# Recommendation head on one core: the last batch tile begins nine units later, label rows and two kinds of loads move

## What is computed

```python
h = concat([q1, q2]) @ w5 + b5
f6 = h @ w6 + b6
g = (v @ v.T)[iu, ju]
f7 = (h[:, iu] * h[:, ju] * g) @ w7 + b7
out8 = concat([f6, f7]) @ w8 + b8
return einsum('bu,bku->bk', out8, label_embedding)
```

## Time and profile before

| | us |
|---|---|
| median of 3 runs | 1762.22 (1760.65 to 1764.42) |
| the profiled execution | 1760.75 |
| its span | 1758.9 |
| TensorE busy | 1583.0 (90% of the span) |
| VectorE busy | 1421.1 (81%) |
| ScalarE busy | 996.4 (57%) |
| GpSimd busy | 137.9 (8%) |
| moved by DMA | 615.20 MB, 350 GB/s over the span |

### The profile page before, as it was taken

The page is one execution under the profiler, slowest core; times in us unless marked ns, Lnnn a source line. Parts: engine busy times, 40 slices in busy tenths (PEclk is TensorE's granted clock), DMA queues, the critical chain, the costliest instruction groups (busy, mean ns, idle before and its releaser), DMA issues.

```text
span 1758.9 us, 25341 instructions
## 1 busy us (share of the span) xinstructions
PE 1583.0 (90%) x7086; PEld 1159.8 (66%) x7086; DVE 1421.1 (81%) x5487; ACT 996.4 (57%) x2931; POOL 137.9 (8%) x96
## 2 busy tenths in 40 slices
PE   2889999999999999999999999899999999998700
PEld 1467677677777777777777777577777777765400
DVE  8897888873898999799998986567777668678956
ACT  7665777764565646464655644344444444433497
POOL 5000000000000000000000000000000000003366
PEclk9999999999999999999999999899999999999955
DMA  7799877977899999999999899999999989999898
GB/s 295 268 390 369 288 273 242 330 279 258 299 332 388 364 409 354 413 357 370 392 359 395 324 393 383 413 358 328 359 381 374 334 314 406 350 357 406 329 397 361
DMA packets 170385, 615.20 MB, mean 350 GB/s; under 512 B 20784, under 2 KB 49421, under 8 KB 162053
## 3 DMA queue, kind: packets, MB, share of 16 engines
q1 hardware_dynamic: 106469, 368.44, 55.0%
q10 hardware_dynamic: 61696, 242.33, 37.0%
q0 software_dynamic: 2080, 2.81, 0.5%
HBM read 609.70 MB, written 3.79 MB: 349 GB/s over the span
## 4 chain that ended last, share of the span: by engine, by line
PE 66%; DMA 15%; DVE 11%; ACT 4%; issue 2%; POOL 1%; SPq 1%; ACTq 0%; DVEq 0%; POOLq 0%
PE bank L706 59%; DMA wring<-in_w7p 8%; DVE stream L1074 5%; DVE cring L1053 3%; DMA stream<-in_x 3%; PE bank L656 3%; DVE junk L953 2%; DMA stream<-in_label 2%; ACT stream L873 2%; PE bank L671 2%; DMA sring<-hrows 1%; ACT wring L862 1%; ACT stage L873 1%; PE bank L684 1%; ACT absjunk L771 1%
## 5 line engine op out<-in xcount | busy, mean ns | idle before, releaser
L706 PE MATMUL bank<-wring,cring 128*128 128x300 f32 (+1 forms) x5616 | 1445.3, 419 | 42.3 <-ACT wring L862 17.3
L706 PEld LDWEIGHTS bank<-wring,cring 128*128 128x128 f32 (+1 forms) x5616 | 1064.6, 191 | 407.2 <-issue 33.5
L862 ACT ACTIVATE wring<-wring,gcol 128x300 f32<-128x300 f32 x1403 | 655.4, 534 | 673.4 <-PE bank L706 579.9
L1053 DVE TENSOR_TENSOR cring<-lefts,sring 128x1024 f32<-128x1024 f32 (+2 forms) x312 | 372.5, 1194 | 190.5 <-PE bank L706 162.2
L1074 DVE SCALAR_TENSOR_TENSOR stream<-stream,out 128x300 f32<-128x300 f32 x1080 | 442.2, 469 | 0.0
L953 DVE SCALAR_TENSOR_TENSOR junk<-stream,ubc 128x300 bf16<-128x300 f32 x784 | 320.5, 469 | 28.3 <-DMA stream<-in_x 28.3
L771 ACT ACTIVATE absjunk<-stream 128x300 bf16<-128x300 f32 x448 | 196.0, 439 | 12.5 <-DMA stream<-in_x 7.1
L1074 DVE DVE_READ_ACCUMULATOR stream<-stream,out 128x1 f32 x1080 | 92.2, 85 | 0.0
L771 ACT ACTIVATION_READ_ACCUMULATOR absjunk<-stream 128x1 f32 x448 | 83.9, 187 | 0.0
L1074 DVE SCALAR_TENSOR_TENSOR stream<-stream,bank 128x300 f32<-128x300 f32 x160 | 64.8, 460 | 22.2 <-DMA stream<-in_label 22.2
L607 POOL DMA_DIRECT2D scores<-score x6 | 3.4, 570 | 987.8 <-DVE stream L1074 829.2
(11 more groups left out here) (94 smaller groups left out, 510.0 us busy)
## 6 DMA issues: line engine op xcount, KB each, us to landing
wring<-in_w7p ACTq DMA_DIRECT2D x365, 600.0 KB, 7.5
stream<-in_label SPq DMA_DIRECT2D x276, 750.0 KB, 10.4
stream<-in_x SPq DMA_DIRECT2D x64, 1050.0 KB, 12.6
sring<-hrows SPq DMA_DIRECT2D x152, 256.0 KB
stage<-in_label SPq DMA_DIRECT2D x44, 750.0 KB, 7.7
wring<-in_w7p ACTq DMA_DIRECT2D x18, 450.0 KB, 5.2
wring<-in_w7p ACTq DMA_DIRECT2D x18, 300.0 KB, 6.5
sring<-hrows SPq DMA_DIRECT2D x96, 44.0 KB
```

The source lines that it names most:

```text
L706: mm = pe.matmul(acc[b % 4][:, 0:E], cring[0:rows, p % CSLOTS, b % 2, j0 + j, :], w, start=(p == BEGIN[b] and j == 0), stop=(p == END[b] - ...
L862: ins = nc.scalar.activation(w, w, ACT.Copy, scale=gcol[:, t:t + 1])
L1053: nc.vector.tensor_tensor(cut(cring, p % CSLOTS, j0), in0, cut(sring, nb % SSLOTS, j0), ALU.mult).then_inc(c_ready, 1)
```

## The change

Four edits:

- `BEGIN[7]` becomes 330 (plus `FIRST_USE` of buffer A6, 51, less 42). In steps 321 to 329 only tile 6 is live, tile 7 runs alone in steps 372 to 422, and `POS` becomes 423. In steps from 372 on VectorE folds `g` into one tile of a unit and no longer into two.
- 130 label rows of tile 6 instead of 80 go into the last steps with units: 130 rows over 40 steps (383 to 422) where 80 went over 31 (383 to 413). The tail has 54 loads instead of 64, of which ScalarE sums 32 instead of 38.
- `H_DONE` becomes 258 instead of 248: label load 139, the first into `stage`, moves from step 250 to 258, and all behind it follow, at most three in two steps, until load 164 stands at its old step 274.
- The first five loads of `w7` are issued by SyncE, behind its x loads, after waits for `g` and for the end of the fold of `w6` and `w8`.

```diff
     BEGIN = [NU * (b // 2) + SHIFT * (b % 2) for b in range(NBT)]
+    BEGIN[-1] += FIRST_USE[KINDS.index(("A", 6))] - SHIFT
...
-        return 0 if len(live(p)) == 2 or n == 1 else min(2, n - 1)
+        return 0 if len(live(p)) == 2 or n == 1 else min(1 if p >= END[-2] else 2, n - 1)
...
-    EARLY_ROWS = 80
+    EARLY_ROWS = 130
...
-    H_DONE = DOTS[NS - 1][1] + LATE[H_OUT] + 1
+    H_DONE = DOTS[NS - 1][1] + LATE[H_OUT] + 11
...
             for q in range(START, STOP):
+                if q == FIRST_W7:
+                    sp.wait_ge(g_ready, 2)
+                    sp.wait_ge(fold_out, NCH)
+                    for p in range(WSLOTS - 1):
+                        a, z = UNIT_TILE[p] * E, UNIT_TILE[p + 1] * E
+                        sp.dma_start(wring[:, p, 0:z - a], w7p[:, a:z]).then_inc(w7_in[p], 16)
...
-                if q == FIRST_W7:
-                    act.wait_ge(g_ready, 2)
-                    for p in range(WSLOTS - 1):
-                        w7_load(p)
```

## The result

| | before | changed |
|---|---|---|
| median, us | 1760.65 (5 runs, 1759.05 to 1764.42) | 1751.32 (5 runs, 1748.61 to 1752.75) |
| profiled span | 1758.9 | 1749.9 |

The ratio is 0.9938, 95% interval 0.9926 to 0.995: 10.9 us faster, 9.3 by the medians. The forecast was 1748, faster, with a range of 1737 to 1763. The time was forecast 3 us too low: of the five terms one (the late slots) was sized from an untypical execution, and one (the first `w7` loads) did not exist. The experiments sort that out.

What follows compares the result with a forecast made beforehand. TensorE was taken to bound the two-tile stretch, DMA bytes the last 208 us. 1758.9 - 1.2 - 11.4 - 16.2 + 33.4 - 17.9 = 1745.6 us of span, 1747.5 with 1.85 around it, forecast 1748, range 1737 to 1763.

Steps and rivals of the forecast that it cites:

- What bounds which stage: Whole kernel: TensorE sets the pace with two tiles live, bytes in the last 208 us, one stall near 1092 apart.
- Late slots, -11.4: Near 1092 us: shifted rows meet an empty queue, saving stall and slow restart, 11.4 us; bounds -11.6 and 0.
- Rival 1: The stall moves: catch-up of 21 label loads delays shifted rows of B4 or later; 1759 us, chance 0.10.
- Nine units alone, -16.2: Steps 321 to 329, only tile 6 live: matmuls -18.2 us, gap +2 us, net -16.2 us.
- Rival 2: The gap is dear: steps 321 to 329 take 3.4 us each; 1759 us, chance 0.08.
- The end stage, +33.4: 51 units with tile 7 alone: 13.7 MB more at 410 GB/s, +33.4 us.
- Rival 3: End stage: shifted rows late, each buffer boundary costing 11.4 us; two of them make 1771 us, chance 0.10.
- rival 5: End stage: TensorE granted only 1.2 GHz, binding the stage, +64 us, 1812 us; chance 0.03.
- The tail, -17.9: After the units: ten loads fewer, -18.4 us by bytes, -17.9 us with ScalarE's work close to DMA's.
- The turn: At about 1660 us, ring full, units done, `out8` not there: 10 us of DMA lost before the change.
- rival 4: The turn shrinks: the 10 us of unfilled DMA there fall away; 1738 us, chance 0.10.
- First `w7` loads, -1.2: At the start: store of `h` lands sooner without `w7` ahead in ScalarE's queue, -1.2 us, between -1.5 and +3.

Runs made afterwards that it cites:

- e2: The kernel before with only `H_DONE` ten steps later (late slots alone): ratio 0.9946, 1749.57 us.
- e3: The kernel before with only the nine units, 130 label rows and the smaller fold: ratio 0.9995, 1759.37 us.
- e7: The changed kernel with `H_DONE` as before, so without the late slots: ratio 0.9989, 1757.96 us.
- e9: The kernel before with only the shifted rows for buffer B2 issued by ScalarE at step 256 instead of SyncE: ratio 1.0022, 1763.14 us.
- e1: The kernel before with only the first five `w7` loads issued by SyncE: ratio 1.0005, 1760.77 us.
- e11: e4 with tile 7 begun eight units later still (17 units alone) and 175 early rows: ratio 0.9988, 1756.55 us.
- e12: The changed kernel itself, measured again on one chip with e13: ratio 0.9931, 1747.86 us.
- e13: e4 once more, on the same chip as e12: ratio 0.9938, 1749.14 us.
- e6: The changed kernel with `g` folded into two tiles of a unit in the end stage, as before, not one: ratio 0.9924, 1746.53 us.
- e4: The changed kernel with the first `w7` loads back on ScalarE: ratio 0.9933, 1747.08 us.
- e5: The changed kernel with 80 early label rows instead of 130: ratio 0.9948, 1750.28 us.
- e10: e4 with four extra matmuls into an unused bank before the first mix of `h`: ratio 0.9934, 1747.44 us.

## Why the prediction was right, and where it was off

**What bounds which stage** held throughout: two tiles by TensorE, the end stage and the tail by bytes, the stall apart. That nearly the whole gain is the stall held too: e2 alone gives 9.5 us of some 11, e3 about 1.

**Late slots, -11.4.** The mechanism was right: e2 takes the stall away, e7 brings it back, and e9 shows that the queue is about half of the delay and the full DMA engines or ScalarE's own loads the rest. The size was that of one execution. The profile of before lost 145.5 - 134.3 = 11.2 us there, but e1, e3 and e7, with the same order of SyncE, lost 9.1, 8.1 and 8.3. VectorE waited 16.0 to 16.5 us in them instead of 18.46, and TensorE stood for 6.1 to 6.6 us instead of 8.61. So the term is 9.2 us on average; the one execution it was read from lay at the high end, where the prediction had put next to nothing above it and did not ask how far below the typical value might lie. Rival 1, that the stall moves, did not happen, though the changed kernel's VectorE did wait 4.5 us at the longest for shifted rows during the catch-up, inside its lead over TensorE. e9 shows what rival 1 looks like.

**Nine units alone, -16.2.** The kernel before spends 164.5 + 192.6 us on the two columns, the changed one 160.4 + 179.6: -17.1 us. The 18.2 us of matmuls left, and the gap cost 1.1 instead of 2. Rival 2 is out for nine units; with 17 (e11) the stretch alone is dear, as that rival feared.

**The end stage, +33.4.** 138.8 - 106.0 = +32.8. The sum by bytes and the one by the queue's half share agreed beforehand and both hold. Rival 3 did not come: VectorE waited for no shifted rows in the stage, and TensorE's waits for ScalarE and VectorE were none over 2.0 us. The granted clock stayed at 1.00 with TensorE 75% busy, so rival 5 is out, too.

**The tail, -17.9.** 80.0 - 99.0 = -19.0. Against the mean of before, e1, e2 and e9 (98.3), -18.3, which is the byte term alone: ScalarE was not late. The turn lost 9 us where it had lost 10; rival 4 is out.

**First `w7` loads, -1.2.** This step failed. It said that the store of `h` was slow because `w7` stood ahead of it in ScalarE's queue. With no `w7` in that queue it took as long (e12, 5.83 us). Where it took 2.8 us, in the changed kernel's first profile, it had been issued 3.8 us later than in e12, when the loads were nearly through. The same happened in e2, whose `w7` loads stood ahead of it in ScalarE's queue: issued late, it landed in 2.7 us. The second store's issue, at which the first one's issue has ended, and the load that waits for the first store, in the changed kernel and in e2:

```profile
71.24 0.73 ACTq L828 DMA_DIRECT2D hrows<-lefts  x1
...
74.10 0.33 SPq L491 DMA_DIRECT2D sring<-hrows  x1
...
70.39 0.51 ACTq L820 DMA_DIRECT2D hrows<-lefts  x1
...
73.14 0.33 SPq L489 DMA_DIRECT2D sring<-hrows  x1
```

So its time follows how much of the loads was still to move when it was issued, and not the queue that they came from. The term can't be told from 0; e1 and the pair e12, e13 agree.

Summed by marks, as means over the kernels with the same code in a stretch: -0.4 (start), -9.2, -17.5, +33.9, -18.8 = -12.0 us; the two ratios of the changed kernel give 10.9 and 12.1. The forecast's terms make -13.3. That the total is off by only 1.3 us is in part luck: late slots and start promised 3.0 us too much, and the other three, which held in their mechanism, together 1.7 too little. The last step of the forecast has a slip of 1 us, too: its sum of 1747.5 plus the 1.5 us between the profiled execution and the median, which it names, is 1749.0 and not 1748. The first profile of the changed kernel differed by 9.0 because it drew 5.4 us more than before's to the first mark. Why that stretch scatters by 11 us was not tried and stays open; the clock in the mix does not explain it: e7 with the full clock needed 1058.1 us, e11 with half of it 1051.5.

No version beats the changed kernel clearly. e6 (1746.53) and e4 (1747.08) have lower medians, each within the interval of the changed kernel's.

## What to carry to other kernels

A burst of large prefetches into newly opened ring slots is paid for by the small urgent transfer behind it; place it behind that transfer, and don't try to rescue one transfer through another queue, since the next one stalls in its place. Where two stages in a row are both full on DMA, moving bytes between them gives nothing, so count the bytes added, not the balance. And read the price of a stall from several executions: this one varied between 8 and 11 us, and the stretches behind it repeated to 1 or 2.

## What was not expected of the hardware

- TensorE's granted clock was 0.5 from 64 to 67 us, in the mix of `h`, in the profiles of the changed kernel, e1, e2, e3, e5 and e11, and 1.00 in those of before, e4, e6, e7, e9, e12 and e13 (and in e10 with its extra matmuls), with the same idle time of about 2.2 and 0.9 us ahead of it in e4 and e2. The mix took 3.7 us or 6.0 to 6.6. The same program had both (changed: 6.27 us, e12: 3.70).
- The first store of `h`, 128 x 128 floats with no `w7` load in its queue, took 5.8 us in e12, where the other queue kept the DMA engines full for the first 3.5 us of it (share 1.05 from 68 to 70 us, 0.96 to 71, 0.61 to 72 and 0.20 to 73). It took 2.8 us in the changed kernel's first profile, issued as the engines emptied (0.93 from 71 to 72 us, 0.23 to 73).
